# A second norm whose mean and eps come out of a product, and a sort that writes the first expert's input already turned

## The reference, cut to what matters

```python
def _layernorm(x):  # eps 1e-5
    return (x - mean(x)) / sqrt(var(x) + eps)
def _smooth_quant_linear(x, w):
    amax_x, amax_w = max|x| over rows, max|w| over rows
    s = sqrt(max(amax_x, EPS) / max(amax_w, EPS))
    x_q, x_scale = round(x / s to 127 per row); w_q, w_scale = round(w * s to 127 per row)
    return x_q @ w_q.T * x_scale * w_scale.T
# x: (4, 256, 256); batch b has its own weights
h = _smooth_quant_linear(_layernorm(x[b]), guw[b]); gate, up = split(h)
x1 = x + tanh(g_xattn) * _smooth_quant_linear(silu(gate) * up, dw[b])
n = _layernorm(x1).reshape(1024, 256)
idx = argmax(softmax(n @ w_gate))            # 8 experts, 128 places each, first come
y[token] = gate[token] * (gelu(n[token] @ w1[idx]) @ w2[idx])   # tokens beyond the places get 0
out = x1 + tanh(g_ffn) * y
```

## Time and profile before

| | us |
|---|---|
| device time, median of 3 runs | 114.49 (113.47 to 117.06) |
| span of the profiled execution, first to last instruction | 110.7 |
| first expert product starts (in the span) | 51.03 |
| last expert product ends | 105.46 |

### The profile page before, as it was taken

One profiled execution on the slowest core, in us unless ns is written; L12 is line 12 of the kernel. 1 busy time (PEld: TensorE's weight loads), 2 busy tenths in 40 slices (PEclk: granted clock), 3 DMA queues, 4 the chain that ended last, 5 costly groups with the idle time before them and its releaser, 6 DMA issues.

```text
span 110.7 us, 2176 instructions
## 1 busy us (share of the span) xinstructions
PE 96.5 (87%) x718; PEld 79.3 (72%) x718; DVE 84.4 (76%) x239; ACT 71.8 (65%) x157; POOL 55.2 (50%) x112
## 2 busy tenths in 40 slices
PE   0996989798598999878989999999999999999910
PEld 0333559597345876657969999999989999898800
DVE  1479989999896599987966497999959669495330
ACT  5005799999899968539537717997849658394000
POOL 6066788766979867864877202122503205050231
PEclk9999999999999999999999999999999999999998
DMA  1999599898943722500379799998999501001011
GB/s 14 298 303 318 205 386 339 309 314 304 312 138 114 265 101 95 190 0 3 101 187 378 253 374 414 333 404 326 324 391 323 177 3 47 0 0 50 0 47 47
DMA packets 14602, 22.65 MB, mean 205 GB/s; under 512 B 1287, under 2 KB 13063, under 8 KB 13568
## 3 DMA queue, kind: packets, MB, share of 16 engines
q1 hardware_dynamic: 13824, 20.46, 54.0%
q0 software_dynamic: 768, 2.07, 5.3%
HBM read 20.46 MB, written 2.10 MB: 204 GB/s over the span
## 4 chain that ended last, share of the span: by engine, by line
PE 53%; DVE 16%; DMA 6%; SPq 5%; ACT 5%; POOL 5%; issue 4%; POOLq 1%; DVEq 0%
PE bk L1382 26%; PE bk L1393 13%; PE bk L1395 6%; DMA gates<-in_g_ffn 6%; DVE am L784 3%; DVE x L864 2%; PE bk L1368 2%; SPq L227 2%; SPq L230 2%; POOL x L407 2%; DVE q1s L792 1%; ACT wide_a L516 1%; POOL sc L374 1%; PE bk L1284 1%; POOLq L34 1%
## 5 line engine op out<-in xcount | busy, mean ns | idle before, releaser
L488 POOL DMA_INDIRECT out<-xrow,sidx x8 | 10.4, 1298 | 36.2 <-DVE xrow L1031 36.2
L1393 PE MATMUL bk<-w2p,hh 128*128 128x512 f32 x64 | 23.5, 407 | 0.1
L1382 PE MATMUL bk<-rows_w,w_sb 128*128 128x128 f32 x192 | 23.1, 276 | 0.2 <-DVE rows_w L973 0.2
L1382 PEld LDWEIGHTS bk<-rows_w,w_sb 128*128 128x128 f32 x192 | 22.2, 192 | 0.8 <-DVE rows_w L973 0.6
L1395 PE MATMUL bk<-w2p,hl 128*128 128x256 f32 x64 | 17.9, 280 | 0.0
L1019 DVE TENSOR_TENSOR hl<-bk,hh 128x512 fp32r<-128x512 f32 x16 | 10.9, 686 | 6.2 <-ACT hh L602 6.0
L581 ACT ACTIVATE w2p<-w_sb 128x1024 fp32r<-128x1024 f32 x12 | 12.1, 1049 | 5.0 <-PE bk L1395 5.0
L1012 DVE TENSOR_TENSOR w2p<-w_sb,w2p 128x1024 fp32r<-128x1024 f32 x12 | 14.4, 1230 | 1.1 <-ACT w2p L581 0.8
L1208 PE MATMUL bk<-identb,upper 128*128 128x512 bf16 x40 | 12.7, 452 | 2.6 <-POOL upper L304 2.6
L1393 PEld LDWEIGHTS bk<-w2p,hh 128*128 128x128 f32 x64 | 12.1, 188 | 2.7 <-issue 0.2
L595 ACT ACTIVATE bk<-bk 128x512 f32<-128x512 f32 x16 | 9.3, 584 | 4.5 <-PE bk L1382 4.5
(11 more groups left out here) (171 smaller groups left out, 214.0 us busy)
## 6 DMA issues: line engine op xcount, KB each, us to landing
w_sb<-in_w SPq DMA_DIRECT2D x12, 1024.0 KB, 6.8
x<-in_x SPq DMA_DIRECT2D x4, 256.0 KB, 4.0
cw<-in_ctx_gu SPq DMA_DIRECT2D x4, 256.0 KB, 4.8
cw<-in_w SPq DMA_DIRECT2D x1, 1024.0 KB, 5.4
out<-x SPq DMA_DIRECT2D x4, 256.0 KB, 2.5
x<-in_w SPq DMA_DIRECT2D x1, 1024.0 KB, 5.0
wide_a<-in_w SPq DMA_DIRECT2D x1, 1024.0 KB, 5.2
wide_b<-in_w SPq DMA_DIRECT2D x1, 1024.0 KB, 7.9
```

The costliest lines, as they stand in the source:

```text
L488: nc.gpsimd.indirect_dma_start(out_rows, bass.IndirectOffsetOnAxis(ap=sidx[:, e:e + 1], axis=0), yo[:, e % 2, :], None, bounds_check=B * T ...
L1382: ins = nc.tensor.matmul(HB[e % 2][:, m, n * C:(n + 1) * C], wv[:, k, f:f + P], xgT[:, e % B, k], start=(k == 0), stop=(k == K - 1))
L1393: nc.tensor.matmul(YB[e % 2], hh[:, e % 2, n], w2p[:, e % 2, n].rearrange("p a d -> p (a d)"), start=(n == 0), stop=False)
```

## The change

Four things are done.

- *Mean and eps as product columns.* `wgc` gets ten columns: 1/256, the eight router weights, -1/256. `x` gets two more columns: column D holds the old mean plus sqrt(256 * eps) (`mean_eps`, a new small DVE instruction per batch) and the last one minus the mean. So `add_x` gives, beside x1, the new mean plus that constant, and minus the new mean. `square2` squares 257 columns, and its sum is 256 * (var + eps) at once. `mean2` is gone, and `rstd2` is one instruction, the power; the factor sqrt(256) is put into the later copies. `square2` now waits for half a batch of x1.
- *Rows normalised ahead of the sort.* `norm2(b, j)` writes (x1 - mean) * rstd, six halves on POOL and two (batch 2 and 3, j = 1) on DVE. `sort` uses these rows as weights and `hot0` as the moving operand, so that its result is already turned; `first_in` and `slots_turn(0)` are gone, and `first_turned` copies one half on DVE and one on ACT.
- *Last expert, low part first.* `last_out_low`, `last_out_high` and `last_add` take the place of `expert_out(7)` and `expert_add(7)`: the product with the low part of w2 goes to a bank of its own, and is added while the rest still runs.
- *Smaller.* `turn5` turns the activations as fp32 from `quantise2`'s result and takes the rounding constant off in ACT's copy, so `round2` on POOL loses an instruction; the bound of the indirect DMAs is a register set once. The lists of all engines are laid anew.

```diff
-        lg = x1[:, :, :, D:D + G]
-        rsd = x1[:, :, :, D + G:H]
-        nm2 = sb("nm2", [P, B, J])
+        lg = x1[:, :, :, D + 1:D + 1 + E]
+        nm2 = x1[:, :, :, D + L - 1]
+        xn2 = rows_w
+        rsd = x1[:, :, :, D + L - 1:H]
...
                 pool.wait_ge(quant2, b + 1)
                 for k in range(K):
-                    nc.gpsimd.tensor_scalar(wd2[:, b, k], qf2[:, b, J + k], -ROUND, q2s[:, b, J + k:J + k + 1],
-                                            ALU.add, ALU.mult)
-                nc.gpsimd.tensor_scalar(qa2[:, b], qf2[:, b, 0:J], -ROUND, 1.0, ALU.add, ALU.mult).then_inc(rounded2, 1)
-
-            def mean2(b):
-
-                pool.wait_ge(x1_ready, b + 1)
-                nc.gpsimd.tensor_tensor(nm2[:, b], x1[:, b, :, D + E], nm1[:, b], ALU.add).then_inc(mean2_ready, 1)
+                    last = nc.gpsimd.tensor_scalar(wd2[:, b, k], qf2[:, b, J + k], -ROUND, q2s[:, b, J + k:J + k + 1],
+                                                   ALU.add, ALU.mult)
+                last.then_inc(rounded2, 1)
 
             def rstd2(b):
 
                 pool.wait_ge(square2_ready, b + 1)
-                link(nc.gpsimd.tensor_scalar(ve2[:, b], ve2[:, b], 1.0 / D, LN_EPS, ALU.mult, ALU.add))
-                link(nc.gpsimd.tensor_tensor(rsd[:, b, :, 0], ve2[:, b], mhalf[:], ALU.pow))
-                nc.gpsimd.tensor_tensor(rsd[:, b, :, 1], nm2[:, b], rsd[:, b, :, 0], ALU.mult).then_inc(shift2_ready, 1)
+                nc.gpsimd.tensor_tensor(x1[:, b, :, D + L], ve2[:, b], mhalf[:], ALU.pow).then_inc(rstd2_ready, 1)
+
+            def norm2(b, j):
+
+                pool.wait_ge(rstd2_ready, b + 1)
+                nc.gpsimd.tensor_scalar(xn2[:, b, j], x1[:, b, j, 0:D], nm2[:, b, j:j + 1], x1[:, b, j, D + L:H], ALU.add,
+                                        ALU.mult).then_inc(norm2_ready, 1)
...
                 act.wait_ge(t5_ready, b + 1)
-                nc.scalar.activation(aT2[:, b], bk[b][:, 0, 0:T // 2].bitcast(BF16), ACT.Copy)
-                nc.scalar.activation(wT2[:, b], bk[b][:, 1, 0:D + G], ACT.Copy).then_inc(moved2, 1)
+                nc.scalar.activation(aT2[:, b], bk[b][:, 0, 0:T], ACT.Identity, bias=-ROUND)
+                nc.scalar.activation(wT2[:, b], bk[b][:, 1, 0:D + L], ACT.Copy).then_inc(moved2, 1)
 
             def square2(b):
 
-                act.wait_ge(x1_ready, b + 1)
-                act.wait_ge(mean2_ready, b + 1)
-                for j in range(J):
-                    last = nc.scalar.activation(wide_a[:, b, j * D:(j + 1) * D], x1[:, b, j, 0:D], ACT.Square,
-                                                bias=nm2[:, b, j:j + 1], accum_out=ve2[:, b, j:j + 1])
+                for j in range(J):
+                    act.wait_ge(x1_ready, J * b + j + 1)
+                    last = nc.scalar.activation(wide_a[:, b, j * (D + 1):(j + 1) * (D + 1)], x1[:, b, j, 0:D + 1],
+                                                ACT.Square, bias=nm2[:, b, j:j + 1], accum_out=ve2[:, b, j:j + 1])
...
+            def first_turned():
+
+                act.wait_ge(sorted_ready, B)
+                nc.scalar.activation(xgT[:, 0, 1], X0[1], ACT.Copy, scale=ROOT_D).then_inc(xgT_ready, 1)
...
-            nc.vector.memset(wgc[:, :, E:G], -1.0 / D)
-            nc.vector.memset(swg[:, :, :, E:G], 0.0)
+            nc.vector.memset(wgc[:, :, 0:1], 1.0 / D)
+            nc.vector.memset(wgc[:, :, L - 1:L], -1.0 / D)
...
+            def mean_eps(b):
+
+                dve.wait_ge(dve_c, done["aggr", b])
+                done["mean_eps", b] = mark(nc.vector.tensor_scalar(x[:, b, :, D], mv1[:, b, :, 0], DELTA, None, ALU.add))
...
-                    ins = nc.vector.scalar_tensor_tensor(out=x1[:, b, j, 0:D + G], in0=bk[b][:, j, 0:D + G],
-                                                         scalar=q2g[:, b, j:j + 1], in1=x[:, b, j], op0=ALU.mult,
-                                                         op1=ALU.add)
-                ins.then_inc(x1_ready, 1)
+                dve.wait_ge(dve_c, max(done["mean_eps", b], done["minus_mean", b]))
+                for j in range(J):
+                    nc.vector.scalar_tensor_tensor(out=x1[:, b, j, 0:D + L], in0=bk[b][:, j, 0:D + L],
+                                                   scalar=q2g[:, b, j:j + 1], in1=x[:, b, j], op0=ALU.mult,
+                                                   op1=ALU.add).then_inc(x1_ready, 1)
...
-            def first_in():
-
-                dve.wait_ge(sorted_ready, B)
-                link(nc.vector.tensor_copy(rs0[:], XD[:, D + G:H]))
-                nc.vector.tensor_scalar(xg[:, 0], XD[:, 0:D], rs0[:, 0:1], rs0[:, 1:2], ALU.mult,
-                                        ALU.add).then_inc(xg_ready, 1)
+            def norm2(b, j):
+
+                dve.wait_ge(rstd2_ready, b + 1)
+                nc.vector.tensor_scalar(xn2[:, b, j], x1[:, b, j, 0:D], nm2[:, b, j:j + 1], x1[:, b, j, D + L:H], ALU.add,
+                                        ALU.mult).then_inc(norm2_dve_ready, 1)
...
-                dve.wait_ge(sidx_ready, 1)
-                dve.wait_ge(xT_ready, 1)
-                nc.vector.tensor_copy(xgT[:, 0].rearrange("p k c -> p (k c)"), XT).then_inc(xgT_ready, 1)
+                dve.wait_ge(sorted_ready, B)
+                nc.vector.tensor_scalar(xgT[:, 0, 0], X0[0], ROOT_D, None, ALU.mult).then_inc(first_ready, 1)
...
+            def last_add():
+
+                e = E - 1
+                dve.wait_ge(last_low_ready, 1)
+                dve.wait_ge(rows_here[e], 16)
+                dve.wait_ge(out_scattered[e % 2], 16 * (e // 2))
+                link(nc.vector.scalar_tensor_tensor(out=yo[:, e % 2], in0=LAST, scalar=gt[:, e:e + 1],
+                                                    in1=gr[:, e], op0=ALU.mult, op1=ALU.add))
+                dve.wait_ge(y_used, e + 1)
+                nc.vector.scalar_tensor_tensor(out=yo[:, e % 2], in0=YB[e % 2][:, 0:D], scalar=gt[:, e:e + 1],
+                                               in1=yo[:, e % 2], op0=ALU.mult, op1=ALU.add).then_inc(y_ready, 1)
...
-                t5 = bk[b][:, 0, :].bitcast(BF16)
-                for j in range(J):
-                    ins = nc.tensor.transpose(t5[:, j * P:(j + 1) * P], qa2[:, b, j], identb[:])
...
-                pe.wait_ge(shift2_ready, b + 1)
-                for j in range(J):
-                    ins = nc.tensor.matmul(XD, hot0[:, b, j], x1[:, b, j], start=(b == 0 and j == 0),
-                                           stop=(b == B - 1 and j == J - 1))
+                pe.wait_ge(norm2_ready, (2, 4, 5, 6)[b])
+                if b >= 2:
+                    pe.wait_ge(norm2_dve_ready, b - 1)
+                for j in range(J):
+                    xv = xn2[:, b, j].rearrange("p (f k) -> p k f", k=K)
+                    for k in range(K):
+                        ins = nc.tensor.matmul(X0[k], xv[:, k], hot0[:, b, j],
+                                               start=(b == 0 and j == 0), stop=(b == B - 1 and j == J - 1))
...
+            def last_out_low():
+
+                e = E - 1
+                pe.wait_ge(y_ready, e - 1)
+                for n in range(NF):
+                    if n % 4 == 0:
+                        pe.wait_ge(w2low_ready, 2 * e + n // 4 + 1)
+                        pe.wait_ge(hhigh_ready, 2 * e + n // 4 + 1)
+                    ins = nc.tensor.matmul(LAST, hh[:, e % 2, n], w2p[:, e % 2, n, 1], start=(n == 0), stop=(n == NF - 1))
+                ins.then_inc(last_low_ready, 1)
+
+            def last_out_high():
+
+                e = E - 1
+                pe.wait_ge(hlow_ready, 2 * e + 2)
+                for n in range(NF):
+                    for a in range(2):
+                        ins = nc.tensor.matmul(YB[e % 2][:, 0:D], (hh, hl)[a][:, e % 2, n], w2p[:, e % 2, n, 0],
+                                               start=(n == 0 and a == 0), stop=(n == NF - 1 and a == 1))
+                ins.then_inc(y_used, 1)
...
-            more_consts()
             rstd1(1)
...
+            more_consts()
             round2(3)
-            mean2(0)
             scales_out(2)
-            mean2(1)
             scales_out(3)
             rstd2(0)
-            mean2(2)
+            norm2(0, 0)
+            norm2(0, 1)
             rstd2(1)
-            mean2(3)
+            norm2(1, 0)
+            norm2(1, 1)
             rstd2(2)
+            norm2(2, 0)
             rstd2(3)
+            norm2(3, 0)
...
             norm1(1)
             norm1(2)
             scale1(0, 1)
             scale1(0, 0)
-            tanh_gates()
             scale1(1, 1)
             scale1(1, 0)
...
+            silu(2)
+            tanh_gates()
             move_row1(3)
+            silu(3)
             scale2(1)
-            silu(3)
...
             onehot_(0)
-            add_x(1)
+            prio_(1)
+            pmax_(1)
             token(0)
+            onehot_(1)
             loc_(0)
             hot0_(0)
-            lmax_(1)
             hotc_(0)
```

(32 more changed lines are left out.)

278 lines of the change are left out of this document (148 added, 130 removed).

## The result

The change makes the kernel faster: 110.16 us (109.87 to 110.36, 4 runs) against 115.44 (113.47 to 117.06, 4 runs) for the kernel before (the three runs known at the prediction and a fourth of 116.38), a ratio of 0.971 with an interval of 0.965 to 0.977. Every ratio here is taken over fast runs alone, without those more than 1.5% above the fastest of their kernel, so it is not the quotient of the two medians. The profiled executions differ by less than the medians, 108.0 against 110.7. There are two reasons. First, the profiled execution of before was one of its shortest: 135 of the 145 executions whose span is known have a device time 1.7 to 2.1 above it, and of 57 executions of the kernel before that were made beside the experiments only one had a span under 110.7. So the 3.8 that the prediction put outside the span were mostly not there.

What follows compares the result with a forecast made beforehand. ACT was taken to pace the front, a chain of dependent steps the routing, PE the experts. Tail -0.52, routing -1.9, front -0.7 and experts +0.1 made -3.0: span 107.7, time 111.5, range 109.9 to 114.1.

Steps and rivals of the forecast that it cites:

- The offset of 3.8: Whole kernel: the median of the runs, 114.49, lay 3.8 above the profiled span, 110.7; added to the forecast span.
- Tail: Behind PE's last product: one of two dependent DVE instructions leaves the path, -0.52; earlier set DMA bound taken as 0.
- Routing: From the last add_x to the first expert product: 4.45 for 6.31, together with the stretch before it -1.9.
- The first half: Routing from the last add_x to the last power's end: 1.5, POOL ending it just as the squares allow.
- the sign which I had named as a disproof: Routing on POOL: a power that waits behind norms would prove the prediction wrong.
- The second half: Routing from the last power to the first product: DVE's one-hot matrices are late, one sort beside them; 0.3 + 2.65.
- Front: Up to the first add_x, paced by ACT: earlier start 0.4 and part of ACT's idle time, -0.7.
- Experts: First two experts: indices gain 1.3, the product 2.6, so the gather's cover of 1.2 is used up; +0.1.
- POOL as the bound: Routing: POOL's norm halves doubled beside DVE's work, last power 2.75 later, time 114.1; chance 0.1.
- The front stalls: Front: waits of silu(3) and the reciprocals make it +0.7 in place of -0.7, time 112.9; chance 0.2.
- gain all it can: Front: the earlier start and all of ACT's idle time, -1.55, time 110.7; chance 0.05.
- The clock falls: PE idle near 30 us and before the experts loses its clock, 5.6 in all, time 117.1; decides at 3.0; chance 0.05.

Runs made afterwards that it cites:

- e2: The changed kernel with the bound of the indirect DMAs given as a number in each again, in place of a register: 110.55 us, 0.971 of the kernel before.
- e4: The changed kernel with expert_out and expert_add for the last expert as for all others: 110.25 us, 0.969 of the kernel before.
- e10: The changed kernel run again, not edited: 110.02 us, 0.966 of the kernel before.
- e5: The changed kernel with norm2(3, 1) moved from DVE to POOL: 110.10 us, 0.967 of the kernel before.
- e1: The kernel before with only the new order of all four engines' lists up to the second product: 113.05 us, 0.997 of the kernel before.
- e3: The changed kernel with scale2(1) ahead of silu(3) on ACT again: 110.40 us, 0.974 of the kernel before.
- e8: The changed kernel with mean_eps behind later reciprocals and gate_up(3, 0) ahead of amax4(0) on DVE: 110.13 us, 0.968 of the kernel before.
- e11: The changed kernel with the old order up to the second product, and mean_eps where DVE waits for PE: 111.78 us, 0.976 of the kernel before.
- e7: The changed kernel with gelu's table loaded ahead of first_turned and hidden_low(0, 0) ahead of split_low(0, 1): 109.94 us, 0.964 of the kernel before.
- e9: The changed kernel with e5's move, gelu's table early, and expert_in(1) ahead of hidden_low(0, 1) on DVE: 109.88 us, 0.963 of the kernel before.
- e6: The changed kernel with both of DVE's norm2 halves moved to POOL: 110.88 us, 0.971 of the kernel before.
- e12: The kernel before with var(1) and norm1(0) ahead of the first weight maximum and bn(2) on DVE: 113.66 us, 0.993 of the kernel before.

## Why the prediction was right, and where not

The sign, the size in the span and, in the main, the mechanism of the largest term were right; three terms were mis-sized, and one number was not what it was taken for. That the sum is only 0.3 off is in part luck: the tail gave 0.54 more than foreseen, routing and front 0.80 less. The time, 110.16, lies near the lower end of the range.

- **The offset of 3.8.** The time was forecast as span plus 3.8: 111.5. The span came out at 108.0 for 107.7; its own device time was 109.87, 1.9 above that span, not 3.8. The difference of 3.8 was between a short execution and a median of longer ones. Had I added 1.9 to the forecast span, it would have been 109.6, 0.6 too low; the two errors went against each other. That the change would also keep PE's clock more often, and so gain more in the median than in the span, was not foreseen.
- **Tail: -1.06 for -0.52.** "I take 0" for the bound of the indirect DMAs was wrong: with the number in the instruction, POOL starts the last scatter 0.80 behind DVE's end, without it 0.28 (e2). The DVE instruction gave 0.41 to 0.45 of the 0.52 that were said (e4). The lag stands in the rows of before (106.50 to 107.30) and I had not priced it.
- **Routing: -1.47 (e10 -1.65) for -1.9.** The first half: the last power ended 1.76 behind `add_x(3)` for 1.5 foreseen, and it waited for POOL's `norm2(2, 0)`, which ended at 45.37, while the squares were done at 45.12. That is the sign which I had named as a disproof; it weighs 0.25. `rstd2(0)` started at 40.08, not 39.6. The second half: 3.08 for 2.95, but not by DVE's `hotc` alone. I counted one sort, 1.16, beside them; PE did two in a row, 2.32, which end when they end, and e5, which relieves DVE, gained nothing clear.
- **Front: -0.33 for -0.7.** The start gave more (-0.69 for -0.4, of which some tenths are the luck of a landing: 11.42 to 11.93), what follows lost 0.36. That `silu(3)` waits was right, that this sets the time was not (e1, e3, e8). And the order does more than the two profiles show: without it the change is some 1.2 slower (e11).
- **Experts: +0.16 for +0.1.** The gather's cover was said to be used up. It wasn't: with a gather that starts 1.15 behind the first product in place of 0.49, PE's stretch does not grow (54.24 in e2). What binds there is DVE's order (e7, e9).

The rivals: *POOL as the bound* did not come by doubling, but is near: two halves more cost 0.6 to 0.8 (e6). The prediction weighed the Trainium skill's factor of two between VectorE and GpSimd ("GPSIMD Engine Reference", section Performance versus the Vector engine): the halves took 0.56 against 0.41 on DVE, 1.4 times, where neither was held up by the other; with two, the sum would have been -2.1, further off. *The front stalls*: not as a whole (-0.33), though what follows its start lost 0.36; nor did it gain all it can. *The clock falls*: not in the change's profiles, but one of its ten executions has a mean clock of 0.964 and a span 1.0 over the median of the others, a third of the 3.0 that would decide. Near 30 us, where I had feared it for the new order, the profiles show it for the old one with `norm1(0)` moved (e12).

## What to carry to other kernels

Read the lag between the last producer and an indirect DMA's start, and keep its bound in a register that is set ahead of the wait. Ask of each wait for a load that stands early in an engine's list which short instruction behind it keeps PE at work, and put that one first; a profile of one execution with an early landing does not show the price. Compare a median with the span of a median execution, never with that of whichever was profiled.

## What the runs showed of the hardware

- An indirect DMA with its bound as a number starts 0.80 and 0.97 behind its data, with the bound in a register 0.28 and 0.30 (e2).
- POOL and DVE hold each other up, and where their norms met it was the later one that took longer. In the change POOL's starts at 46.26 and takes 0.56, DVE's at 46.36 and takes 0.60 for 0.41; in e10 it is the other way round:

```profile
46.36 0.69 POOL L414 TENSOR_SCALAR rows_w<-x 128x256 f32<-128x256 f32 x1
46.29 0.41 DVE L980 TENSOR_SCALAR rows_w<-x 128x256 f32<-128x256 f32 x1
```

- Beside `hotc`, whose two inputs lie in SBUF, a POOL half took 0.82 (e6); beside `hot0`, which reads one from PSUM, 0.56 (e5 and e6, 46.91 and 46.71). The Trainium skill ("GPSIMD Engine Reference", section Specifications) says that the SBUF interfaces are shared with VectorE, with contention for DVE instructions with two SBUF inputs or in a 2-port perf mode; these rows agree for the two inputs, and which mode DVE's norm ran in no row shows.
- The granted clock fell to its lower level (a reading of 0.50) in a single idle time of PE of 2.30 (e11, 0.66 from 9.5 to 10.0), and during the last of three shorter ones of 0.46, 0.56 and 0.65 (e12, 0.73 from 29.0 to 29.5); it held over the same three in the profiled executions of before and e11, and over one of 1.39 (the change).
